# A fused attention and FFN layer: the first batch's load order, early V projections, a split first stack, and two FFN chunks moved ahead

## What is computed

```
x: 8 batches x 512 rows x 256 columns, float32; 16 heads of width 16
q, k, v = x @ Wq + bq, x @ Wk + bk, x @ Wv + bv
y  = softmax(causal(q k^T / 4)) v                    # per head
h  = layernorm(x + y @ Wo + bo)
g  = silu((h @ fp8(gate_w)) * gate_scale)            # 256 -> 768
u  = (h @ fp8(up_w)) * up_scale
out = layernorm(h + ((g*u) @ fp8(down_w)) * down_scale)   # 768 -> 256
```

## Time and profile before

| | us |
|---|---|
| median of 3 runs | 561.79 |
| lowest and highest | 561.22, 562.51 |
| the profiled execution, its own time | 561.78 |
| its span in the trace | 560.0 |
| outside the span | 1.78 |

### The profile page before, as it was taken

How to read it: one execution, slowest core, us unless ns; L and a number is a source line. 1 busy time by engine, 2 the same in 40 slices (tenths; PEclk the granted TensorE clock), 3 DMA queues, 4 the chain that set the end, 5 groups by cost and what they waited for, 6 DMA issues and landing times.

```text
span 560.0 us, 10677 instructions
## 1 busy us (share of the span) xinstructions
PE 531.7 (95%) x3921; PEld 356.8 (64%) x3921; DVE 458.7 (82%) x808; ACT 315.2 (56%) x579; POOL 226.5 (40%) x251
## 2 busy tenths in 40 slices
PE   8789899999999999999999999997899999999992
PEld 4345465665656656666666565563488888888892
DVE  7877588898988888889889898986748888888876
ACT  3046467666576675766766667664653554345530
POOL 5015233434443533434443453340425653455542
PEclk9888899999999999999999999997999999999997
DMA  5968665756554577556564664400000101110012
GB/s 181 262 165 271 162 181 156 179 187 172 175 172 128 183 198 199 164 135 187 157 173 153 139 200 152 123 4 2 1 0 1 39 1 39 39 38 27 12 39 75
DMA packets 61516, 68.19 MB, mean 122 GB/s; under 512 B 6296, under 2 KB 55832, under 8 KB 61464
## 3 DMA queue, kind: packets, MB, share of 16 engines
q1 hardware_dynamic: 60632, 66.59, 41.0%
q10 hardware_dynamic: 832, 0.92, 0.5%
HBM read 37.62 MB, written 29.61 MB: 120 GB/s over the span
## 4 chain that ended last, share of the span: by engine, by line
PE 83%; DVE 6%; issue 4%; DMA 3%; ACT 2%; POOL 1%; POOLq 0%; DVEq 0%; SPq 0%; ACTq 0%
PE ps L1110 16%; PE ps L964 11%; PE ps L972 10%; PE ps L859 10%; PE ps L1119 7%; PE ps L945 7%; PE ps L925 5%; PE ps L946 5%; PE ps L867 5%; PE ps L897 2%; DVE nmax L613 2%; PE ps L908 1%; PE ps L990 1%; DMA m_scratch<-mrow 1%; ACT probs L446 1%
## 5 line engine op out<-in xcount | busy, mean ns | idle before, releaser
L613 DVE TENSOR_REDUCE nmax<-ps 128x2 f32<-128x1024 f32 (+1 forms) x192 | 196.8, 1040 | 50.2 <-PE ps L946 49.7
L446 ACT ACTIVATE probs<-ps 128x512 f32<-128x512 f32 x320 | 183.9, 597 | 81.1 <-PE ps L964 79.8
L370 POOL TENSOR_SCALAR_AFFINE_SELECT probs<-probs 128x512 f32<-128x512 f32 x128 | 87.0, 693 | 213.1 <-ACT probs L446 213.1
L964 PE MATMUL ps<-q_st,k_st 98*128 98x384 bf16 (+3 forms) x512 | 123.6, 305 | 5.7 <-ACT probs L446 3.1
L397 POOL TENSOR_TENSOR f_l<-f_full,f_h 128x512 fp32r<-128x512 f32 x48 | 63.5, 1324 | 73.6 <-ACT f_h L529 73.6
L945 PE MATMUL ps<-k_st,q_st 98*128 98x256 bf16 (+2 forms) x384 | 83.0, 277 | 5.4 <-DMA k_st<-k_scratch 3.5
L946 PE MATMUL ps<-k_st,q_st 124*128 124x128 bf16 x512 | 84.7, 221 | 0.0
L972 PE MATMUL ps<-probs,v_st 128*32 128x512 f32 (+3 forms) x1024 | 83.9, 444 | 0.2
L964 PEld LDWEIGHTS ps<-q_st,k_st 98*128 98x128 bf16 x512 | 44.6, 99 | 51.1 <-issue 27.3
L524 ACT ACTIVATE sgate<-ps,s_gate 128x512 f32<-128x512 f32 x48 | 32.8, 685 | 60.0 <-PE ps L1110 60.0
L946 PEld LDWEIGHTS ps<-k_st,q_st 124*128 124x128 bf16 x512 | 46.2, 98 | 18.8 <-DVE nmax L613 13.7
(11 more groups left out here) (96 smaller groups left out, 832.9 us busy)
## 6 DMA issues: line engine op xcount, KB each, us to landing
q_st<-q_scratch SPq DMA_DIRECT2D x32, 384.0 KB
k_st<-k_scratch SPq DMA_DIRECT2D x32, 384.0 KB
q_scratch<-part SPq DMA_DIRECT2D x16, 384.0 KB, 3.7
k_scratch<-part SPq DMA_DIRECT2D x16, 384.0 KB, 2.6
xT<-in_attn_xT SPq DMA_DIRECT2D x8, 512.0 KB, 3.8
q_scratch<-part SPq DMA_DIRECT2D x16, 256.0 KB, 3.8
resid<-in_attn_x SPq DMA_DIRECT2D x8, 512.0 KB, 3.9
k_scratch<-part SPq DMA_DIRECT2D x15, 256.0 KB, 2.1
```

Source lines behind the costliest of these rows:

```text
L370: pool.affine_select(out=blocks, in_=blocks, compare_op=ALU.is_ge, fill=0.0, base=0, pattern=[*pattern, [1, P]], channel_multiplier=-1).th ...
L446: act.activation(probs[:, u, :], ps[:, u % 2, :], ACT.Exp, scale=SCALE).then_inc(exp_done, 1)
L613: dve.tensor_reduce(nmax[:, i, heads[0]:heads[-1] + 1], src, AX.X, ALU.max, negate=True).then_inc(max_taken, 1)
L964: m = pe.matmul(ps[:, u % 2, c0:c0 + T - P * j], k_st[0:RP, g, h, P * j:P * j + P], q_st[0:RP, g, h, P * j:T], start=True, stop=True)
```

## The change

**Start.** `load_xT(1)` goes ahead of the stores of batch 0. TensorE projects V of batch 1 too (`project_v(1, 0)` and `(1, 1)` into banks 0 and 1) before the first scores, and eight zero matmuls stand where twelve did. VectorE fills the constant columns of `v_st` earlier and empties four V tiles in place of two. The first stack is loaded as two halves of two heads; `scores_max(0, 0)` and `(0, 2)` each wait for theirs. Window 3 loses its V work.

**Loads.** `load_x(0)`, `load_raw(0)`, `load_x(1)` and three scale loads no longer stand ahead of the stores of batch 1. `load_x(n+1)` and `load_raw(n)` (n below 3) now close SP's loop of batch `n`; `load_x(0)` follows `load_stack(1, 1)`.

**Work on VectorE and POOL.** Quantisation begins in window 5, three steps a window; windows 30 and 31 take 11 and 10. `norm_in(0)` and `norm_in(1)` move from the end of window 29 into window 28. `add_bias(n)` moves from group 1 to group 3, in the last batch from window 29 to window 31, right behind the first mask.

**FFN.** `gate_up(0, 0, 0)` stands behind `scores(31, 7)` and `gate_up(0, 0, 1)` ahead of `attend_rest(31)`; the remaining four stay behind it.

The diff, cut to its core:

```diff
@@ queue of SP
             sp.dma_start(b_v[:], bv.partition_broadcast(P)).then_inc(const_in, 16)
+            load_xT(1)
             store_parts(0, 0)
...
             sp.wait_ge(mask_filled, 3)
-            load_stack(0, 0)
+            for k in range(2):
+                sp.wait_ge(part_stored[k], 48)
+            for v in range(2):
+                rows, heads = slice(32 * v, 32 * v + 32), slice(2 * v, 2 * v + 2)
+                sp.dma_start(q_st[RM:RP, 0, heads], q_scratch[rows].rearrange("(h d) a t -> (d a) h t", d=D)).then_inc(half_loaded[v], 16)
+                sp.dma_start(k_st[RM:RP, 0, heads], k_scratch[rows].rearrange("(h d) a t -> (d a) h t", d=D)).then_inc(half_loaded[v], 16)
             load_stack(0, 1)
-            load_xT(1)
...
-                    load_x(0)
-                    load_raw(0)
                 if nxt:
-                    load_x(n + 1)
                     store_parts(n + 1, 0)
...
-                if n in (1, 3):
-                    load_raw((n + 1) // 2)
+                if n == 0:
+                    load_x(0)
...
                     load_stack(n + 1, 2)
+                    load_x(n + 1)
+                if n < 3:
+                    load_raw(n)
@@ POOL
-                    if g == 1:
+                    if g == 3:
                         add_bias(n)
@@ DVE
-                return 3 * (w - 2) + 3 * max(w + 2 - W, 0)
+                return 3 * (w - G - 1) + 8 * max(w + 2 - W, 0)
...
             empty_v(0, 1, MB)
+            for v in range(2):
+                empty_v(1, v, v)
...
-                    if w > 1:
+                    if w > G:
                         quantize(first_step(w))
+                    if last_n and g == 0:
+                        norm_in(0)
...
-                        for q in range(3):
+                        for q in range(8 if w + 1 < W else 7):
                             quantize(first_step(w) + 3 + q)
-                    if last_n and g == 1:
-                        norm_in(0)
-                        norm_in(1)
@@ PE
             project_v(0, 1, None, MB)
-            keep_warm(12)
+            for v in range(2):
+                project_v(1, v, None, v)
+            pe.wait_ge(v_out, 2)
+            keep_warm(8)
...
+                if w == 0 and u in (0, 2):
+                    pe.wait_ge(half_loaded[u // 2], 32)
...
-                elif n + 1 < B and g == 3:
+                elif 0 < n < B - 1 and g == 3:
                     project_v(n + 1, i, half)
...
                     scores(w, 7)
+                    if w + 1 == W:
+                        pe.wait_ge(max_taken, NM * W)
+                        pe.wait_ge(mT_out, W)
+                        pe.wait_ge(quant, 8 * NQ * 2 // 3)
+                        gate_up(0, 0, 0)
...
+                    if w + 1 == W:
+                        gate_up(0, 0, 1)
...
-            gate_up(0, 0, 0)
             transpose_y(W - 1)
-            gate_up(0, 0, 1)
+            gate_up(0, 0, 2)
             transpose_yn(B - 1, 1)
-            gate_up(0, 0, 2)
+            gate_up(0, 0, 3)
             project_o(B - 1, 0)
-            gate_up(0, 0, 3)
+            gate_up(0, 0, 4)
             project_o(B - 1, 1)
-            gate_up(0, 0, 4)
             gate_up(0, 0, 5)
```

More of the change, by code:

```diff
@@ L532, in _ @@
                 for ic in range(IC):
-                    if n == 0 and ic == 2:
+                    if n == 0 and ic == 3:
                         empty_ynT(B - 1, 1, MB)
@@ L874, in project_v @@
                     take_bank(n, "v", v)
+                if not half:
+                    pe.wait_ge(xT_loaded[n % 2], (n // 2 + 1) * 16)
                 project(half, v, xT[:, n % 2], w_v, v_full, bank)
```

90 lines of the change are left out of this document (51 added, 39 removed).

## The result

The changed kernel takes 556.93 us (median of 4 runs, 555.70 to 557.76) against 562.15 for the kernel before (4 runs): a ratio of 0.989, 95% interval 0.987 to 0.992. The forecast was 555.5 with a range of 549.0 to 559.5. The profiled run took 557.38 us, span 555.7; the one of before had a span of 560.0. So its trace has 4.3 us to explain, where the sum said 6.3, and the medians 5.2.

The account below looks back on a forecast made before the run. TensorE was taken as the bound, full in the FFN and most of attention, losing time at three waits and the slow clock behind them. From 561.78 us, -1.5 -3.2 -2.2 +0.3 +0.4 -5.9 +5.7 +0.1 gave 555.5, range 549.0 to 559.5.

Parts of the forecast that it names:

- Start, -1.5: Before the first scores: TensorE starts 1.1 us sooner and at full clock, 1.5 us won, bounded by 0 and 2.8.
- VectorE's chain of reductions carries it on: Step of the start term: the 1.5 us won before the first reduction is passed on by VectorE's reductions.
- Window 2, -3.2: Window 2: the 2.1 us wait for its maxima and 1.7 of slow clock go, less 0.6 for the next stack.
- Window 3, -2.2: Window 3: without V's four pieces it falls from 11.40 to no less than 9.2 us; bounds 1.5 and 3.5.
- Later loads, +0.3: Ends of batches 0 to 2: maxima of windows 5, 9 and 13 queue behind the moved loads; 0.3 us lost, bounds 0 and 2.
- slower rival: Loads collide at three batches' ends, so windows 5, 9 and 13 each lose 3.8 us: 566.6 us; chance 0.06.
- Windows 28 and 29, +0.4: Eight norm_in among window 28's reductions make window 30's maxima late, so transpose_max(30) waits 0.4 us.
- Window 30, -5.9: Window 30: with norm_in early, its stretch of 14.03 us should look like window 31's 8.13.
- Window 31, +5.7: Window 31: first_hT(1, 1) stalls 4.0 us for VectorE's steps, one held by POOL's bias, then 1.7 lost at half clock.
- 0.3 for each meeting: Windows 30 and 31: a VectorE step beside a POOL mask lengthens by 0.3 us; by that alone stall 1.8, total 551.6.
- Chunks, +0.1: Two FFN chunks moved ahead fill 0.8 us of idle time and waits, against 0.7 for ScalarE's copy and a 0.2 wait.
- slow stretch of window 0 goes as well: Rival: the start's shift keeps the clock up in window 0, from 39.12 to 45.60; 3.2 us more won, 552.3; chance 0.12.

Follow-up runs that it names:

- experiment 6: Changed kernel with the old start: 560.37 us, or 558.85 without a wait left in by mistake; with only the first stack loaded whole: 554.99 us.
- experiment 4: Changed kernel with the residual, scale and raw weight loads back ahead of the stores of the next batch's parts: 560.40 us.
- norm_late: Changed kernel with norm_in(0) and norm_in(1) back at the end of window 29: 561.12 us.
- experiment 2: Changed kernel with three of the eight quantisation steps at the end of window 30 moved to the end of window 31 (five and ten): 551.10 us.
- steps_even: Changed kernel with five and ten quantisation steps at the ends of windows 30 and 31 in place of eight and seven: 551.10 us.
- experiment 5: Changed kernel with the first two gate_up chunks back behind the last scores and the statements around them at their old chunks: 556.30 us.
- three_edits: Changed kernel with the last batch's bias in window 29, five and ten quantisation steps, and batch 0's parts 2 and 3 stored by group: 550.62 us.
- experiment 1: Changed kernel with the last batch's output bias added by GpSimd in window 29 instead of window 31: 552.06 us.

## Why the prediction was right, and which terms were not

The time and the sign were right, 1.4 us from the median. The terms, against the trace of the changed kernel and the experiments:

- **Start, -1.5: wrong, too little of it is left to be measured.** The local part held. TensorE's first scores came at 22.08, at full clock, against the forecast 20.7; the first projections ended 1.4 us later in this trace, and less that it is 20.7. The first reduction moved from 22.82 to 22.72 with the same 1.4 in it. The step that failed is "VectorE's chain of reductions carries it on". The chain isn't the last thing to end. `scores_max(2, 0)` needs the stack of group 2, which SyncE issues when all stores of parts 2 and 3 have landed: 14.0 us behind the first stack in the kernel before (15.94 to 29.95), 14.5 in the changed one (17.33 to 31.79). The transfers between them run one behind another and are no fewer. The issue of that stack and `scores_max(2, 0)`, changed and then before:

```profile
31.79 0.32 SPq L248 DMA_DIRECT2D q_st<-q_scratch  x1
38.04 0.42 PE L970 MATMUL ps<-k_st,q_st 98*128 98x384 bf16 x1 [3.23 <-DMA k_st<-k_scratch]
...
29.95 0.32 SPq L240 DMA_DIRECT2D q_st<-q_scratch  x1
36.30 0.32 PE L945 MATMUL ps<-k_st,q_st 98*128 98x384 bf16 x1 [1.06 <-DVE nmax L613]
```

  Both start 6.3 us behind the issue. In the kernel before a reduction is named as the last to end, so the row of that wait alone didn't show how near the stack was; the 6.3 us do. In the changed kernel's trace TensorE stood 3.2 us for the stack and then ran at half clock. A second, smaller step failed too: "the earlier memsets ... hide" is not so where the projections come early (0.5 us, experiment 6). Old and new start, measured apart, differ by 1.9 us of medians, no more than V's 2.1 in window 3 (experiment 6).
- **Window 2, -3.2: right,** -3.17, by the mechanism given (experiment 4). The wait for the next stack that was to cost 0.6 is there, 0.60 at 60.55. In the trace of before the wait was followed by half clock; in experiment 4 it was not, but there the wait itself was 2.9 and the next stack cost 1.3. The loads' old places cost 3.2 to 3.8 in window 2 in both traces, and how that splits differs.
- **Window 3, -2.2: right,** -2.39; the window takes 9.01 us, 0.2 below the floor of 9.2.
- **Later loads, +0.3: too small,** 1.0 in windows 4 and 5. "No slack" was right for window 5 (the maxima were stored at 83.53 and their load issued at 89.30), but the wait for them is only 0.2. The other 0.6 is `scores_max(6, 0)` for its zero rows, behind the same loads. I had followed only the maxima through the queue, not the stack. Experiment 4 puts 0.6 of the 1.0 on the loads; the rest of window 4 stays without them. In windows 9 to 14 most traces of kernels with the same loads show losses of 0.2 to 1.3 in one or two windows, the changed kernel's and `norm_late`'s none: the slower rival's collision exists, but at about a third of its price at most and never in all three places.
- **Windows 28 and 29, +0.4:** 0.17.
- **Window 30, -5.9: right,** 5.7 (scores to scores 14.03 to 8.34), shown by experiment 3.
- **Window 31, +5.7: right in kind, 0.6 too large.** The stall is 3.7 for 4.0, the clock's part 1.4 for 1.7, both read by experiment 2. The clock's part is some luck: it was 2.3 in two other traces with the same wait. That the step waits until POOL's instruction ends was inferred from one `norm_in` piece (it happened to seven, 1376 to 1391 ns); here it took 2.38 us and ended 0.2 behind the bias. The masks' rows were misread. By "0.3 for each meeting" the stall would have been 1.8, but 0.3 is no price of a meeting: it is all that is left of a mask of 0.6 to 0.7 us when a step starts in it. Read by their ends, those rows say the same as the `norm_in` pieces and as the sentence of the Trainium skill (SBUF — State Buffer, "SBUF: two separate sides"); the rows are in the last section. A step that passes POOL's instruction at 0.3 is in none of them.
- **Chunks, +0.1: right where the stall is gone.** In steps_even window 31 and all behind it take 9.1 + 158.0 = 167.1 us, in the kernel before 8.1 + 159.1 = 167.2. Beside the stall it is open (experiment 5).

The errors were of both signs. Against the traces the sum had 2.3 too much gain at the start (1.4 of it the late projections, which are chance), 0.7 too little loss for the loads, and some 1 us too much loss at the end and in windows 28 and 29; the trace ended 1.9 us from the sum. That only 1.4 are left against the median is luck in part: the errors cancel, and the half clock behind the stall stayed short. The rival "slow stretch of window 0 goes as well" did not occur in the changed kernel. When the group-wise stores removed the wait for the stack, the clock stayed up. But the waits that the rival names, for reductions, are not shown to bring the half clock: in the kernel before one of 1.06 us at 36.30 stood ahead of it, in three_edits one of 0.97 at 34.96 did not bring it.

## What to carry to other kernels

When work is pulled forward, ask what each consumer behind it waits for *last*: here two gains (earlier first scores, then the earlier stack of group 2) arrived at a chain of transfers that had not moved. Nothing that can be told was left of the first, and in the traces 2.4 of the second's 4.4 us. The row of a wait names only the release that came last; the one just behind it is found by timing it from its own issue. When steps of VectorE are moved, look at which of them will meet a long instruction of GpSimd, not only at how many there are: three steps fewer were worth 5 us, since they also kept the queue out of a meeting of 2 us. To learn whether an instruction waits for another engine, compare the two ends, not the lengthening. In this kernel a wait of TensorE of 3 us or more is to be priced from its own length to 2.3 us above it.

## What the runs showed of the hardware

- **Who is held beside GpSimd, and until when.** A TENSOR_SCALAR of VectorE, float32 from and to SBUF, 0.36 us alone, took 2.38 beside an addition of 2.44 on POOL. Another, from fp8 (0.35 at its shortest), took 0.67 beside a mask of 0.71. Both ended 0.2 us behind POOL's instruction. The trace of the kernel before had this already, in 26 quantisation steps that start while a mask runs and are more than 0.08 us longer than the shortest of their kind: the 13 TENSOR_SCALAR ones all end 0.21 us behind their mask, the 13 with two SBUF inputs all 0.41 behind. One of the first kind, and its mask (the mask ends at 99.74, the step at 99.95):

```profile
99.36 0.59 DVE L582 TENSOR_SCALAR q_t<-w_raw 128x384 f32<-128x384 f32 x1
99.10 0.64 POOL L370 TENSOR_SCALAR_AFFINE_SELECT probs<-probs 128x512 f32<-128x512 f32 x1 [1.59 <-ACT probs L446]
```

```profile
4.96 1.96 PE L877 MATMUL ps<-xT,w_q 128*128 128x512 f32 x4
```

```profile
5.75 2.71 PE L878 MATMUL ps<-xT,w_q 128*128 128x512 f32 x4
```

  The first is `norm_late` (experiment 3), the second the changed kernel. SyncE issues the first store at 10.41 us in the one and at 11.44 in the other (10.04 in the kernel before). So one trace of each kernel can't judge an edit of the start; the first `attend` of six kernels with one and the same start stood between 43.96 and 47.17.
- **A wait doesn't always bring the half clock, nor always as much of it.** All waits of 3.2 us or more in these traces were followed by it, one of 2.9 (experiment 4) was not. Of the shorter ones before `scores_max(2, 0)` in window 0, those of 1.1 to 2.7 us were followed by it, one of 1.7 in window 31 (experiment 1) was not. Behind one and the same wait of 3.7 us, window 31 takes 14.2 us in four traces (mean clock 0.88) and 15.1 in two (0.77). What decides it is open.
